# GpSimd in ScalarE's place for the scaling of a layer norm, in a two-layer gated transformer block

## The reference

```
def _layernorm(x, axis=-1, eps=1e-05):
    m = jnp.mean(x, axis=axis, keepdims=True)
    v = jnp.var(x, axis=axis, keepdims=True)
    return (x - m) / jnp.sqrt(v + eps)
...
    x = x + jnp.tanh(g_xattn[0]) * _L0_xattn_ref(ctx_1024, _layernorm(x, axis=-1), ...)
    x = x + jnp.tanh(g_ffn[0]) * _L0_ffn_ref(_layernorm(x, axis=-1), ...)
    x = x + jnp.tanh(g_xattn[1]) * _L1_xattn_ref(_layernorm(x, axis=-1), ctx_1024, ctx_1024, ...)
    x = x + jnp.tanh(g_ffn[1]) * _L1_ffn_ref(_layernorm(x, axis=-1), ...)
```

## Time and profile before

| what | value |
|---|---|
| median of 3 runs | 694.24 us (692.23 to 704.61) |
| the profiled execution | 694.52 us, of which the span is 692.5 us |
| TensorE busy | 627.4 us, 91 percent of the span |
| ScalarE busy | 370.3 us, 53 percent |
| VectorE busy | 369.4 us, 53 percent |
| GpSimd busy | 138.0 us, 20 percent |
| mean granted clock of TensorE | 0.954 |

### The profile page before, as it was taken

One profiled execution on the slowest core, in us unless ns is written; L12 is line 12 of the kernel. 1 busy time (PEld: TensorE's weight loads), 2 busy tenths in 40 slices (PEclk: granted clock), 3 DMA queues, 4 the chain that ended last, 5 costly groups with the idle time before them and its releaser, 6 DMA issues.

```text
span 692.5 us, 10248 instructions
## 1 busy us (share of the span) xinstructions
PE 627.4 (91%) x3676; PEld 479.1 (69%) x3676; DVE 369.4 (53%) x817; ACT 370.3 (53%) x631; POOL 138.0 (20%) x206
## 2 busy tenths in 40 slices
PE   2698988988799999999999999999889789999996
PEld 2574555544378788888888777787567667888885
DVE  6677667767573523425546435434477655343332
ACT  4326747565865845646557435545756564243232
POOL 8433264243640000000000000001245212000000
PEclk9869999999999999999999999999988799999999
DMA  7321120112022030110303340000253000000000
GB/s 223 99 72 26 32 60 9 47 49 94 2 58 96 0 122 0 57 66 0 123 16 77 80 134 2 1 1 2 59 171 94 2 3 1 1 30 1 31 31 30
DMA packets 21969, 34.66 MB, mean 50 GB/s; under 512 B 4640, under 2 KB 13216, under 8 KB 21920
## 3 DMA queue, kind: packets, MB, share of 16 engines
q1 hardware_dynamic: 19648, 30.51, 14.3%
q0 software_dynamic: 1984, 3.44, 2.1%
q10 hardware_dynamic: 288, 0.07, 0.1%
HBM read 18.93 MB, written 2.10 MB: 30 GB/s over the span
## 4 chain that ended last, share of the span: by engine, by line
PE 77%; DVE 10%; ACT 5%; issue 4%; POOL 4%; DVEq 0%; ACTq 0%; POOLq 0%
PE SC L1157 28%; PE PV L1157 26%; PE AUX L1157 5%; PE PV L1175 5%; PE SC L1290 4%; PE AUX L1262 4%; DVE NM L1041 2%; ACT XN L752 2%; PE AUX L1218 2%; DVE O L1049 2%; DVE ST L959 1%; PE PV L1262 1%; POOL RSTD L626 1%; POOL QG L655 1%; PE AUX L1340 1%
## 5 line engine op out<-in xcount | busy, mean ns | idle before, releaser
L901 DVE TENSOR_TENSOR HL<-HF,HH 128x512 fp32r<-128x512 f32 x120 | 83.6, 696 | 155.9 <-ACT HH L847 155.6
L805 ACT ACTIVATE PB<-SC 77x1024 f32<-77x1024 f32 x96 | 94.2, 1014 | 45.2 <-PE SC L1290 45.0
L847 ACT ACTIVATE HH<-PV 128x512 fp32r<-128x512 f32 x96 | 57.3, 596 | 66.9 <-PE SC L1157 66.8
L842 ACT ACTIVATE HF<-PV 128x512 f32<-128x512 f32 x96 | 57.3, 597 | 57.0 <-PE PV L1157 54.9
L626 POOL TENSOR_TENSOR RSTD<-RSTD,NHALF 128x4 f32<-128x4 f32 x16 | 17.8, 1112 | 325.5 <-DVE RSTD L972 325.4
L1157 PE MATMUL PV<-XH,WAH 128*128 128x512 f32 x192 | 78.1, 407 | 1.1 <-DVE O L1049 1.1
L1157 PE MATMUL PV<-XL,WAH 128*128 128x512 f32 x192 | 76.4, 398 | 0.0
L1157 PE MATMUL PV<-XH,WAL 128*128 128x512 f32 x192 | 76.3, 397 | 0.0
L1157 PE MATMUL SC<-HL,WBH 128*128 128x512 f32 x192 | 75.6, 394 | 0.0
L1157 PE MATMUL SC<-HH,WBH 128*128 128x512 f32 x192 | 75.4, 392 | 0.0
L1157 PE MATMUL SC<-HH,WBL 128*128 128x512 f32 x192 | 75.0, 391 | 0.0
(11 more groups left out here) (229 smaller groups left out, 1217.7 us busy)
## 6 DMA issues: line engine op xcount, KB each, us to landing
QG<-QH SPq DMA_DIRECT2D x96, 64.0 KB, 2.0
WSA<-in_wa SPq DMA_DIRECT2D x6, 1024.0 KB, 5.0
WSB<-in_wb SPq DMA_DIRECT2D x12, 512.0 KB, 6.6
QG<-QL SPq DMA_DIRECT2D x48, 64.0 KB, 2.0
X<-in_x SPq DMA_DIRECT2D x4, 512.0 KB, 6.4
QG<-QH POOLq DMA_DIRECT2D x32, 64.0 KB, 2.2
out_x<-X SPq DMA_DIRECT2D x4, 512.0 KB, 2.6
QG<-QL POOLq DMA_DIRECT2D x16, 64.0 KB, 2.1
```

Source lines behind the costliest of these rows:

```text
L805: act.activation(probs(n)[0:S, :, :], SC[0:S, n % 2, :, :], ACT.Exp, scale=SCALE[a]).then_inc(exp_done, 1)
L842: act.activation(HF[s % 2][:, :], PV[:, s % 2, :], ACT.Gelu_apprx_tanh)
L847: act.activation(HH[s % 2][:, :], PV[:, s % 2, :], ACT.Gelu_apprx_tanh).then_inc(act_done, 1)
L901: return dve.tensor_tensor(dst, raw, hi.bitcast(F32), ALU.subtract)
```

## The change

ScalarE's part of the step `("scale", ...)` is taken out and GpSimd gets one. The four ACTIVATE instructions become four TENSOR_SCALAR instructions (times the scale of the row, plus its offset), with the same inputs and the same output, the same two waits, and the same count on xn_ready. PLAN is unchanged, and so is the step's place in it.

```
+                elif kind == "scale":
+
+                    _, stage, j = step
+                    n = order[step]
+                    pool.wait_ge(rstd_ready, n + 1)
+                    if n:
+                        filled(pool, ("turn",) + NORMS[n - 1][1:] + (KC - 1,))
+                    for t in range(TT):
+                        ins = pool.tensor_scalar(XN[:, t, :], X[:, TT * j + t, :], RSTD[:, 1, t:t + 1], RSTD[:, 3, t:t + 1],
+                                                 ALU.mult, ALU.add)
+                        if t < TT - 1:
+                            ins.then_inc(pool_step, 1)
+                            chain += 1
+                    ins.then_inc(xn_ready, 1)
...
-                elif kind == "scale":
-                    _, stage, j = step
-                    n = order[step]
-                    act.wait_ge(rstd_ready, n + 1)
-                    if n:
-                        filled(act, ("turn",) + NORMS[n - 1][1:] + (KC - 1,))
-                    for t in range(TT):
-                        ins = act.activation(XN[:, t, :], X[:, TT * j + t, :], ident_f, scale=RSTD[:, 1, t:t + 1],
-                                             bias=RSTD[:, 3, t:t + 1])
-                    ins.then_inc(xn_ready, 1)
```

## The result

The changed kernel takes 709.04 us (median of five, 706.33 to 716.78) against 695.24 us for the kernel before on the same chip (five, 692.23 to 704.61). The ratio is 1.0221 with a 95% interval of 1.0156 to 1.0287: slower by 15.4 us of 695. The ratio is worked out from the fast runs of each kernel (those within 1.5% of its fastest), and not as the quotient of the two medians (1.0198). The forecast was 701.6 us with a range of 697 to 706, so the direction was right and the size was about half of what came.

The account below looks back on a forecast made before the run. TensorE bounds the kernel, busy 627.4 of 692.5 us. Terms 7.15 + 0.15 - 0.1 - 0.3 + 0.75 - 0.3 = 7.35 us on the profiled 694.52 give 701.9, so 701.6 us against the median; range 697 to 706.

Parts of the forecast that it names:

- Norm 0, +7.15 us: Program start: scaling queues behind thirteen small DMAs on GpSimd, delaying TensorE's first transpose 7.15 us, all reaching the end.
- rival 3: Start: a later step waits for something unmoved and absorbs 4.4 us of the delay, giving 697.4 us; chance 0.06.
- the zones were to begin some 7 us later: Sign: TensorE's unbroken feed-forward stretch through the chosen zones begins some 7 us after 192 us.
- The transpose was promised at 20.3 to 20.5: Sign at the start: TensorE's first transpose at 20.3 to 20.5 us instead of 13.21, with matching idle time before it.
- The copies of QG behind norm 11: Six GpSimd copies land 2.2 us later, at 504.1; TensorE wants them at 504.56: cost nothing, otherwise under 1 us.
- Norm 6, -0.3 us, ends -2.1 and +0.6: First attention: tile 0.15 to 0.6 us later, but an exponential wait can go; net gain 0.3 us.
- Norms 12 to 14, +0.75 with norm 11: TensorE idles during scaling: 0.15 us each, norm 12 perhaps 0.3; sum 0.75, less 0.3 for norm 11's exponentials.
- Norms 1 to 5, 7 to 10 and 15: Norm 1 costs 0.15 us, norm 2 gains 0.1; the others, mostly under unbroken TensorE work, nothing.
- TensorE's clock: First 50 us, mean granted clock 0.85: lower-level stretches could move the start a microsecond or two either way.
- Rival 1: ScalarE's relief, 16.6 us at norms 2 to 6 and 11 to 13, wins: 686 to 691 us, not slower; chance 0.08.
- 33 forecast: Sign in the changed profile: about 33 us less busy time on ScalarE and 35 us more on GpSimd.
- Rival 2: GpSimd contends with VectorE, slowing scalings at norms 1, 6, 11 to 14: 704.5 to 712 us; chance 0.12.

Follow-up runs that it names:

- only0_small_behind: Kernel before with norm 0 alone scaled on GpSimd and the thirteen small DMAs issued behind that scaling: ratio 1.0018 (0.9982 to 1.0054).
- only0: Kernel before with norm 0 alone scaled on GpSimd, the other fifteen on ScalarE: 701.61 us, ratio 1.0092 (1.0046 to 1.0137).
- only11: Kernel before with norm 11 alone scaled on GpSimd: 702.96 us, ratio 1.0090 (1.0048 to 1.0132).
- before_copies_late: Kernel before, all norms on ScalarE; GpSimd also computes norm 11's scaled tiles, unread, before its six QG copies: 702.25 us, ratio 1.0115.
- only1to10: Kernel before with norms 1 to 10 scaled on GpSimd, norms 0 and 11 to 15 on ScalarE: ratio 1.0007 (0.9975 to 1.0039).
- covered_only: Kernel before with norms 1 to 5, 7 to 10 and 15 scaled on GpSimd, the others on ScalarE: ratio 0.9997 (0.9964 to 1.0031).
- after_filled: Whole change plus identity transposes on TensorE while it waits for XN at norms 6 and 11 to 14: 702.17 us, ratio 1.0132 against the kernel before.
- no0_no11: Kernel before with all norms but 0 and 11 scaled on GpSimd: ratio 1.0050 (1.0018 to 1.0081).
- the side-by-side run: Kernel before with TensorE's waits filled by identity transposes, without and with norms 1 to 5, 7 to 10, 15 on GpSimd: ratios 0.9954 and 0.9941.
- both_mended: Whole change, with norm 0's scaling before the thirteen small DMAs and QG copies before norm 11's scaling: 703.22 us, ratio 1.0100 against the kernel before.
- before_filled: Kernel before plus identity transposes on TensorE (11, 22, 22, 6) in its waits at norms 11 to 14: ratio 0.9975 (0.9937 to 1.0012).

## Why the prediction was wrong

- **Norm 0, +7.15 us: right.** Measured 6.65 us at the first transpose and 0.92% or 6.4 us (3.2 to 9.5) at the end by itself. The mechanism (thirteen DMAs in front, nothing absorbs it) held, and only0_small_behind shows the order as its cause; rival 3, the absorbed start, falls with only0. On the way the lag was not steady: the zones were to begin some 7 us later, and norm 7's transposes came 13.2 us later in the change and 11.8 in only0, at a lower clock. The half microsecond too much is that GpSimd's product ended at 10.43 and not at 10.96. The transpose was promised at 20.3 to 20.5 and came at 19.86, in only0 at 20.04.
- **The copies of QG behind norm 11, costed at nothing with 0.4 us of slack, "if that cover is gone ... under 1 us": this is the step that failed.** The issue times were right (a shift of 1.9 us measured, 2.0 forecast). The landing was wrong: I took the 2.2 us of the page's median, a figure over all 32 copies, for six copies that the shift moves into the loads of WI. Their worst landing is 6.8 to 7.3 us. The wait that came of it is 3.4 to 4.1 us from transpose to maximum, and the whole cost 0.90% in only11 and 1.15% in before_copies_late, 6 to 8 us against none. With 6.3 us in the sum the forecast would have been 707.9, within the spread of the runs. The question that was not asked: which other transfers are in flight at the new time? The trace of the kernel before had SyncE's WI right behind GpSimd's last copy at 499.31:

```profile
499.35 0.53 SPq L581 DMA_DIRECT2D WI<-in_wg  x1
```

- **Norm 6, -0.3 us, ends -2.1 and +0.6: wrong sign.** The wait grew by 0.91 us, more than the upper end, because GpSimd's product took 0.44 us for 0.20 and the scaling 2.59 us for 2.08. The wait for an exponential at 184.70 did not vanish to the change's credit. The cost is below what only1to10 can show.
- **Norms 12 to 14, +0.75 with norm 11:** the waits grew by 0.87, 0.20 and 0.19 us. Norms 13 and 14 are as forecast (0.15 each) and norm 12 is three times its 0.3; by themselves they are not measurable (0.9996).
- **Norms 1 to 5, 7 to 10 and 15: right,** covered_only 0.9997.
- **TensorE's clock was named as the least firm point, but for the start alone and for 1 to 2 us.** The start itself kept its clock (0.86 in the first 56 us, where it was 0.85 in 50). It fell around norms 12 to 14 and behind norm 6, and after_filled puts about 0.9% on it for the whole change. The forecast had no term and no rival for clock lost behind the longer waits of the second attention, where the earlier trace rows show 0.87. This is the second term that was put at nothing: without norms 0 and 11 the sum has 0.35 us, and no0_no11 measured 0.50%, 3.5 us (1.3 to 5.6), of which the longer waits of norms 6 and 12 to 14 are 2.2 us.
- **Rival 1 (ScalarE's relief)** falls: 27.9 us less of ScalarE (33 forecast), and no gain in covered_only or in the side-by-side run. **Rival 2 (contention)** had a true mechanism at a size that matters little: eight of the sixteen groups took 2.59 to 3.19 us, which makes GpSimd's 40.4 us out of the forecast's 35, but six of the eight lie where TensorE doesn't wait, and covered_only, with all six of these, costs nothing that shows. Norm 6's took 2.59 us and norm 12's 2.87. Its time of 704.5 to 712 holds the result for another reason; that is luck.

## What to carry to other kernels

When work moves onto a queue that also issues DMAs, list every DMA behind it, find its new time, and look for what else is in flight then: take the landing from copies that run beside such loads, not the program's median. A step that goes to another engine does so in front of that engine's queue or behind it, and this one choice was worth 0.7% here; an engine with 20% of load can still be the wrong one. Where TensorE has to wait for one to four microseconds again and again, cheap transposes in the gap can be worth more than the hand-over that one wants to shorten, but it has to be measured for each gap.

## What the runs showed of the hardware

- **GpSimd can stand still beside VectorE.** In only0_small_behind the four scalings took 3.79 us for 2.16. The line's own view has least, middle and most in ns:

```profile
L639 POOL TENSOR_SCALAR XN<-X,RSTD x4: 553/554/2173, 10.8 to 14.0; 128x256 f32<-128x256 f32 x4
```

  Three took 554 ns, and one 2173. At that time VectorE was running two-input subtractions:

```profile
9.68 1.83 DVE L916 TENSOR_TENSOR WDL<-WKR,WDH 128x768 fp32r<-128x768 f32 x2 [0.85 <-ACT WDH L724]
```

  In both_mended, with those subtractions from 10.94 on, the group took 4.60 us. ScalarE's scaling beside the same work takes 2.07 us. So the order that mends norm 0 has a price of its own, 1.6 us, which moving the DMAs behind can't remove. The Trainium skill (GPSIMD Engine Reference, Key points) names contention with VectorE's two-input instructions, without a size; the trace agrees, and the size here is up to 1.6 us for a single instruction.
- **Idle time and lower clock go together, but not one for one.** Filling the waits for XN raised the mean clock from 0.935 to 0.955 in the changed kernel and from 0.949 to 0.955 in the kernel before; filling the wait for the copies left it at 0.941.
- **One kernel's own runs spread with the clock:** of the kernel before, the runs of one experiment at a mean clock of 0.952 to 0.959 took 691.78 to 695.74 us, those at 0.930 to 0.935 700.53 to 700.78 us. Effects of half a percent needed twelve runs. A single trace can mislead in the same way: before_filled does not differ from the kernel before in front of norm 11, yet its profiled execution had a mean clock of 0.60 from 146 to 186 us and reached norm 6's transposes 6.6 us later (186.01 and 179.42).
